# Six of eight experts take their tokens by an indirect DMA, one more weight chunk per expert stays unsplit, and the expert weights lie in runs of 8 KB

## What is computed

```
probs = softmax(LN(x) @ gate_w.T + gate_b)        # 8 experts
w_te  = the two largest probs of a token, else 0
per expert e:
    tok = the 93 tokens with the largest w_te[:, e]
    xg  = LN(x)[tok]                              # 93 x 512
    h   = gelu(xg @ w1[e] + b1[e])                # w1[e]: 512 x 2048
    y   = (h @ w2[e] + b2[e]) * w_te[tok, e]      # w2[e]: 2048 x 512
    x[tok] += y
```

## Time and profile before

| | us |
|---|---|
| runs | 2076.36, 2076.19, 2075.21 |
| profiled execution, its own time | 2075.6 |
| its span, first to last instruction | 2073.9 |
| TensorE (PE) busy | 2054.4 (99%) |
| VectorE (DVE) busy | 1485.4 (72%) |
| ScalarE (ACT) busy | 1139.5 (55%) |
| GpSimd (POOL) busy | 931.0 (45%) |
| granted TensorE clock | 1.000 |
| DMA | 201.15 MB, 97 GB/s over the span |

### The profile page before, as it was taken

The page is one execution under the profiler, slowest core; times in us unless marked ns, Lnnn a source line. Parts: engine busy times, 40 slices in busy tenths (PEclk is TensorE's granted clock), DMA queues, the critical chain, the costliest instruction groups (busy, mean ns, idle before and its releaser), DMA issues.

```text
span 2073.9 us, 36144 instructions
## 1 busy us (share of the span) xinstructions
PE 2054.4 (99%) x13385; PEld 1927.0 (93%) x13385; DVE 1485.4 (72%) x3088; ACT 1139.5 (55%) x3030; POOL 931.0 (45%) x707
## 2 busy tenths in 40 slices
PE   8999999999999999999999999999999999999998
PEld 7986666788899999999999999999999999999997
DVE  8769999744676766676767676676767676766776
ACT  4566777524655554555555555445555555554464
POOL 0010001301565655555555555555656565655461
PEclk9999999999999999999999999999999999999999
DMA  5205999900322111111122211111111222111110
GB/s 143 89 23 171 325 349 314 304 31 9 126 81 75 65 66 66 66 66 66 65 82 94 87 66 66 66 66 66 66 66 66 95 84 82 66 66 66 62 47 25
DMA packets 89162, 201.15 MB, mean 97 GB/s; under 512 B 8197, under 2 KB 12581, under 8 KB 88986
## 3 DMA queue, kind: packets, MB, share of 16 engines
q1 hardware_dynamic: 86746, 196.28, 27.7%
q0 software_dynamic: 2240, 2.57, 0.5%
HBM read 196.31 MB, written 2.51 MB: 96 GB/s over the span
## 4 chain that ended last, share of the span: by engine, by line
PE 95%; DVE 4%; ACT 1%; DMA 0%; issue 0%; POOL 0%; SPq 0%; DVEq 0%
PE PS L54 86%; PE PS L57 5%; PE PS L53 5%; DVE LW L60 1%; DVE JU L76 1%; DMA X<-in_x 0%; DVE OHsx L68 0%; DVE ACC L60 0%; DVE SM L107 0%; DVE XFL L60 0%; DVE OHdx L69 0%; DVE PO L68 0%; DVE U L69 0%; DVE W1L L60 0%; DVE GEL L60 0%
## 5 line engine op out<-in xcount | busy, mean ns | idle before, releaser
L54 PE MATMUL PS<-ZH,WS 128*128 128x314 f32 x4096 | 939.7, 310 | 0.0
L54 PEld LDWEIGHTS PS<-ZH,WS 128*128 128x128 f32 x4096 | 695.7, 189 | 0.0
L54 PE MATMUL PS<-ZL,WS 128*128 128x314 f32 x2048 | 626.9, 306 | 0.0
L60 DVE TENSOR_TENSOR ACC<-ACC,PS 128x314 f32<-128x314 f32 x1008 | 462.6, 476 | 196.9 <-PE PS L54 186.8
L60 POOL TENSOR_TENSOR WS<-RAW,WS 128x512 fp32r<-128x512 f32 x256 | 326.7, 1298 | 167.6 <-ACT WS L88 167.6
L54 PEld LDWEIGHTS PS<-ZL,WS 128*128 128x128 f32 x2048 | 387.0, 189 | 0.0
L60 POOL TENSOR_TENSOR ML<-MF,MH 128x400 fp32r<-128x400 f32 x124 | 129.7, 1046 | 428.5 <-ACT MH L88 428.5
L88 ACT ACTIVATE ZH<-PS,g1T 128x628 fp32r<-128x628 f32 x128 | 100.7, 787 | 255.0 <-PE PS L54 255.0
L60 POOL TENSOR_TENSOR WQ<-RAW,WQ 128x512 fp32r<-128x512 f32 x128 | 217.6, 1700 | 42.9 <-ACT WQ L88 42.9
L88 ACT ACTIVATE EE<-EE,SM 125x100 f32<-125x100 f32 x640 | 233.4, 379 | 1.2 <-DVE SM L68 1.2
L88 ACT ACTIVATE MH<-MF 128x400 fp32r<-128x400 f32 x128 | 68.3, 533 | 286.7 <-DVE MF L60 285.5
(11 more groups left out here) (366 smaller groups left out, 3650.1 us busy)
## 6 DMA issues: line engine op xcount, KB each, us to landing
RAW<-in_L_ffn_wz_w SPq DMA_DIRECT2D x66, 1024.0 KB, 5.3
RAW<-in_L_ffn_w SPq DMA_DIRECT2D x64, 1024.0 KB, 7.3
RAW<-in_L_ffn_Wq_w SPq DMA_DIRECT2D x32, 1024.0 KB, 5.5
CB<-c_rows SPq DMA_DIRECT2D x32, 195.3 KB
RAW<-in_L_gnn_W SPq DMA_DIRECT2D x4, 1024.0 KB, 16.1
RAW<-in_L_ffn_Wkv_w SPq DMA_DIRECT2D x4, 1024.0 KB, 15.1
RAW<-in_L_ffn_Wk_T SPq DMA_DIRECT2D x2, 1024.0 KB, 18.5
WB<-w_rows SPq DMA_DIRECT2D x6, 273.4 KB
```

The costliest lines, as they stand in the source:

```text
L54: return self.q.matmul(o, l, r, start=start, stop=stop)
L60: return Nothing() if self.q is None else self.q.tensor_tensor(out=o, in0=a, in1=b, op=op)
```

## The change

The diff, cut to its core; the tiles `XG` (94 x 2 x 512, over the place of `XFL`), `IX` and `TOK` are new.

```diff
-                srcs.append(I["L0_ffn_w1"][e, :, 512 * c:512 * c + 512].rearrange("(k p) n -> p k n", p=128))
+                srcs.append(I["L0_ffn_w1"][e, c])
-                srcs.append(I["L0_ffn_w2"][e, 512 * c:512 * c + 512, :].rearrange("(k p) n -> p k n", p=128))
+                srcs.append(I["L0_ffn_w2"][e, c])
...
-            return m % 8 < (7 if m < 8 * NE - 8 else 6)
+            return m % 8 < 6
...
-            return 7 * (m // 8) + m % 8
+            return 6 * (m // 8) + m % 8
...
@@ sp_moe, before the loop of loads
+            q.dma(xrow[0:1, :], ZR[:, :]).then_inc(s_wrow, 16)
+            q.wait_ge(*xfh_done.of(4, "u"))
+            for lo, hi in ((0, 120), (120, 125)):
+                q.dma(xrow[1:626, :].rearrange("(t p) d -> p t d", p=P)[lo:hi], MU[lo:hi, :, :]).then_inc(s_wrow, 16)
@@ g_moe
+            q.iota(TOK[:, :], [[P, T5]], 1).then_inc(*mconst.up("token"))
+            q.wait_ge(*mconst.of("token"))
+            q.ts(WSP[:, :, :, 2], TOK[:, :].unsqueeze(2).broadcast_to([P, T5, 8]), 1.0, None, ALU.add)
+            q.fill(WSP[:, :, :, 3].bitcast(f32), 0.0).then_inc(*mconst.up("code"))
...
+            q.wait_ge(s_wrow, 80)
+            for e in range(NP_, NE):
+                q.wait_ge(*sw_v.of(e, "row"))
+                q.wait_ge(*(xg_t.of(e - 2) if e >= NP_ + 2 else ga_mm.of(NP_ - 1)))
+                if e > NP_:
+                    q.wait_ge(s_rows, 16 * (e - NP_))
+                q.gather(XG[:, e % 2, :], xrow, IX[:, e % 2:e % 2 + 1]).then_inc(s_rows, 16)
+            q.wait_ge(s_rows, 16 * (NE - NP_))
@@ a_moe
-                q.wait_ge(*ga_mm.of(e))
-                q.act(OT[:, :], PS[0:CS, 6, :], ACT.Copy).then_inc(*ga_done.up(e))
+                if e < NP_:
+                    q.wait_ge(*ga_mm.of(e))
+                    q.act(OT[:, :], PS[0:CS, 6, :], ACT.Copy).then_inc(*ga_done.up(e))
...
             for e in range(NE):
-                n = 7 * e
+                n = 6 * e
...
-                weights(n + 10)
                 scale(e)
@@ v_moe
+            def places_of(e):
+                k = e % 2
+                q.wait_ge(*sw_mm.of(e))
+                if e > NP_ + 1:
+                    q.wait_ge(s_rows, 16 * (e - NP_ - 1))
+                q.cp(IX[:, k:k + 1], PS[0:CS, 4, 2:3]).then_inc(*sw_v.up(e, "row"))
...
                 q.wait_ge(*gelu_a.of(e, c))
+                q.wait_ge(s_wrow, 80)
...
             for e in range(NE):
-                n = 7 * e
+                n = 6 * e
+                if NP_ <= e + 1 < NE:
+                    places_of(e + 1)
                 weights(n + 4)
                 gelu(e, 0)
+                if NP_ <= e + 1 < NE:
+                    dispatch(e + 1)
...
-                if e == 0:
-                    gelu(e, 2)
-                if e and split(8 * e + 6):
-                    gelu(e, 2)
...
-                weights(n + 10)
@@ pe_moe, dispatch
+                if e >= NP_:
+                    return
...
+            def places_of(e):
+                k = e % 2
+                q.wait_ge(*rank_v.of(e, "po"))
+                q.wait_ge(*gate_v.of("wsl"))
+                q.wait_ge(*mconst.of("code"))
+                q.wait_ge(*free[4])
+                for t in range(T5):
+                    i = q.mm(PS[0:CS, 4, 0:4], PO2[:, k, t, :], WSP[:, t, e, :], t == 0, t == 4)
+                i.then_inc(*sw_mm.up(e))
+                free[4] = sw_v.of(e, "two")
@@ pe_moe, gathered_T
-                q.wait_ge(*ga_done.of(e))
+                if e < NP_:
+                    q.wait_ge(*ga_done.of(e))
+                else:
+                    q.wait_ge(s_rows, 16 * (e - NP_ + 1))
...
+                rows = OT[:, :] if e < NP_ else XG[:, e % 2, :]
...
             for e in range(NE):
+                if NP_ <= e + 1 < NE:
+                    places_of(e + 1)
                 up(e, 0)
@@ kernel, on the host
+        if name == "L0_ffn_w1":
+            a = _np.ascontiguousarray(a.reshape(8, 4, 128, 4, 512).transpose(0, 3, 2, 1, 4))
+        if name == "L0_ffn_w2":
+            a = _np.ascontiguousarray(a.reshape(8, 4, 4, 128, 512).transpose(0, 1, 3, 2, 4))
```

More of the change, by code:

```diff
@@ L1174, in program @@
         YH = at("YH", [P, T5, D], f32, after("HW3"))
+        XG = at("XG", [CS, 2, D], f32, after("XFH"))
+        IX = at("IX", [CS, 2], i32, after("XG"))
         LG = at("LG", [P, T5, 8], f32, after("XFL"))
@@ L1177, in program @@
         WM = at("WM", [P, T5, 8], f32, after("GS"))
-        WSP = at("WSP", [P, T5, 8, 2], f32r, after("WM"))
+        WSP = at("WSP", [P, T5, 8, 4], f32r, after("WM"))
         RKA = at("RKA", [P, 8, T5], f32, after("WSP"))
@@ L1183, in program @@
         IH = at("IH", [P, T5], i32, after("IL"))
-        c4 = at("c4", [P, 2, T5, 64], f32, after("IH"))
+        TOK = at("TOK", [P, T5], f32, after("IH"))
+        c4 = at("c4", [P, 2, T5, 64], f32, after("TOK"))
         CD = [at(f"CD{k}", [P, 6, T5], f32, after("IH") + 128 * k) for k in range(3)]
@@ L1243, in program @@
         wrow = nc.dram_tensor("w_rows", (8, 625), f32, kind="Internal").ap()
-        NB = 6
+        NB, NP_ = 6, 2
+        xrow = nc.dram_tensor("x_rows", (626, D), f32, kind="Internal").ap()
         yrow = nc.dram_tensor("y_rows", (1 + NB * CS, D), f32, kind="Internal").ap()
@@ L1322, in g_moe @@
             q.fill(io94[:, CAP:CS], -1.0).then_inc(*mconst.up("all"))
+            q.wait_ge(*mconst.of("all"))
+            q.iota(TOK[:, :], [[P, T5]], 1).then_inc(*mconst.up("token"))
+            q.wait_ge(*mconst.of("token"))
+            q.ts(WSP[:, :, :, 2], TOK[:, :].unsqueeze(2).broadcast_to([P, T5, 8]), 1.0, None, ALU.add)
+            q.fill(WSP[:, :, :, 3].bitcast(f32), 0.0).then_inc(*mconst.up("code"))
             q.wait_ge(*x1_done.of(4))
@@ L1577, in rank_end @@
                 if e >= 2:
-                    q.wait_ge(*ga_mm.of(e - 2))
+                    q.wait_ge(*sw_mm.of(e - 2))
+                    if e - 2 < NP_:
+                        q.wait_ge(*ga_mm.of(e - 2))
+                    if e - 2 >= NB:
+                        q.wait_ge(*pt_t.of(e - 2))
                 for t in range(T5):
@@ L1592, in dispatch @@
                     q.wait_ge(*os_hi.of(e - 2))
-                q.cp(sw[k][:, 0:2], PS[0:CS, 7, 0:2]).then_inc(*sw_v.up(e, "two"))
+                b = 7 if e < NP_ else 4
+                q.cp(sw[k][:, 0:2], PS[0:CS, b, 0:2]).then_inc(*sw_v.up(e, "two"))
                 q.wait_ge(*sw_v.of(e, "two"))
                 q.tt(sw[k][:, 2:3], sw[k][:, 0:1], sw[k][:, 1:2], ALU.add).then_inc(*sw_v.up(e, "sum"))
+            def places_of(e):
[4 more added lines that the diff above has]
+                q.cp(IX[:, k:k + 1], PS[0:CS, 4, 2:3]).then_inc(*sw_v.up(e, "row"))
             def gathered_T(e):
@@ L1614, in scale @@
                 q.wait_ge(s_b2[k], 32 * (e // 2 + 1))
-                q.wait_ge(*ga_done.of(e))
-                q.wait_ge(*xg_t.of(e))
-                if e + 1 < NE:
-                    q.wait_ge(*xg_t.of(e + 1))
+                q.wait_ge(*ga_done.of(NP_ - 1))
+                q.wait_ge(*xg_t.of(NP_ - 1))
+                if e:
+                    q.wait_ge(*os_hi.of(e - 1))
                 q.tt(OT[:, :], PS[0:CS, 2, :], B2[:, k, :], ALU.add).then_inc(*ot_v.up(e))
@@ L1654, in back_low @@
             def back_low():
-                q.wait_ge(s_rows, 16 * T5)
+                q.wait_ge(s_rows, 16 * (NE - NP_ + T5))
                 for t in range(T5):
@@ L1720, in v_moe @@
                     gathered_T(e + 1)
-                    dispatch(e + 1)
+                    if e + 1 < NP_:
+                        dispatch(e + 1)
                 weights(n + 9)
@@ L1751, in pe_moe @@
             q.wait_ge(*w_hi.of(0, 1))
-            pe_busy(q, 3, HW[1], 17)
+            pe_busy(q, 3, HW[0], 17)
             turned(0)
@@ L1874, in pe_moe @@
             q.wait_ge(*free[7])
-            pe_busy(q, 7, HW[1], 19)
+            pe_busy(q, 7, HW[0], 19)
             rank_row(0)
@@ L1878, in pe_moe @@
             q.wait_ge(*free[2])
-            pe_busy(q, 2, HW[1], 21)
+            pe_busy(q, 2, HW[0], 21)
             dispatch(0)
@@ L1966, in a_counts @@
         def a_counts(q):
-            q.wait_ge(*w_used.of(chunk(7 * NE - 4)))
+            q.wait_ge(*w_used.of(8 * NE - 5))
             for m in range(T5):
@@ L1972, in v_counts @@
             for m in range(T5):
-                q.wait_ge(*w_used.of(chunk(7 * NE - (3 if m < 4 else 2))))
+                q.wait_ge(*w_used.of(8 * NE - (4 if m < 4 else 3)))
                 q.wait_ge(*gch_done.of(m))
```

20 lines of the change are left out of this document (9 added, 11 removed).

## The result

The changed kernel took 2086.11 us, the median of six runs (2081.92 to 2090.87), against 2076.19 us (2075.21 to 2077.01) for the kernel before: a ratio of 1.0049, with a 95% interval of 1.0039 to 1.0059. It is 9.9 us slower. The forecast was 2067.0 us, and its range ended at 2073.0, so it was wrong in sign and in size. The profiled execution took 2087.79 us, with a span of 2086.0.

The account below looks back on a forecast made before the run. TensorE was taken to bound the kernel, with DMA and VectorE right behind. The terms -13.9 + 4.7 - 0.9 + 1.0 = -9.1 us against the profiled 2075.6 gave 2066.5, stated as a median of 2067.0; range 2064.5 to 2073.0.

Parts of the forecast that it names:

- What goes from TensorE, what comes: TensorE's order: gathering products go in experts 2 to 7 (13.9 us), chunk 6 unsplit in seven experts adds 4.7 us.
- the stall: First expert: PE's 0.87 us wait for XGL before expert 1's first product was taken as gone, 0.9 us saved.
- The gather: New indirect DMA of token rows: lands before the transposes need it, 0 us, bounds 0 and 1 us per expert.
- ScalarE's loads: Second rival: hidden tile 3's copy waits behind a high part whose chunk load lands late; 2083.6 us, chance 0.06.
- the rival's 17.5 us: Second rival's size: with landings of 11.8 us PE stops 2.5 us in each of seven experts; chance 0.06.
- Both ends: Start and end of the stage: new instructions, token writes and later loads stay hidden, 0 us, at worst 2 us each.
- The cover: End of the stage: Wk_T loads land 2.9 us before TensorE wants them, shrinking to some 1.3 us; 0, at worst 2.
- The granted clock: PE's clock was 1.00 in all windows, the 2.4 GHz level, and no change was expected.
- the tight point: DMA per expert: 9.24 MB need 26.7 us against a period of 25.6, or 25.1 us with the long-run layout.
- The 1.0 us of the sum: Loss over the whole stage for loads landing late on busy DMA; bounds 0 and 1.1 us for each of six experts.
- Third rival: The gather lands beyond T + 21.8 in the expert, so PE waits for it: 2074 to 2077 us, chance 0.05.
- The signs: Wrong if spacing exceeds 26.3 us, PE waits for HS, LW or XGL in each expert, or idles after 388 us for Wk_T or X.

Follow-up runs that it names:

- the kernel in which nothing is late: Changed kernel with gathers padded to 96 rows for XG and 128 for YL and YH, runs of 8 KB, chunk 6 unsplit: 2066.09 us, ratio 0.9945.
- the fastest kernel: Changed kernel with 96 rows for XG, 128 for YL and YH, and seven of eight chunks split as before the change: 2063.06 us, ratio 0.9939.

## Why the prediction was wrong, point by point

**What goes from TensorE, what comes: right.** The products taken out (13.9 us), the unsplit chunks (4.7) and the stall (0.9) make 10.1 us. 2076.2 - 10.1 = 2066.1, and the kernel in which nothing is late took 2066.09, with a period of 25.52 us for the 25.6 forecast. That it fits to 0.1 us is luck, since its parts are off by more: the unsplit chunk with its order cost 2.9 for 3.8, and the products, by the two kernels with chunk 6 unsplit and nothing waited for inside the experts, 2079.40 - 2066.09 = 13.3 for 13.9. The counts came as forecast: 128 records of RAW,GT in the stage (72 before), and products of XFH and XFL in experts 0 and 1 alone.

**The gather: the step that failed.** The prediction said "I take 0, bounds 0 and 1 us per expert". It priced the gather by its bytes ("0.19 MB is a seventh of five YH gathers"), as a smaller YH, and asked only when its own rows would be there. For the rows themselves that bound held in the changed kernel, even with a landing of 15.0 us: TensorE waits for no XG. What it left out is what the gather does to others while it lasts: 94 rows go to two DMA engines, with 47 rows each, as the packets show; the 1 MB loads in flight beside it land late, and the reading that fits is that they wait for their part on those engines. So 7.3 us became 10.1. The sum had nothing for this, and the row count, 2 x 47, was there to be asked about. Undoing this alone, by two rows, gives 13.9 us of the 19.

**ScalarE's loads: mechanism right, weight wrong.** It named the place (the copy of hidden tile 3 behind the high part), the allowance of 9.3 us from issue to landing and the landing from which the kernel would be slower, 10.7. The trace shows this wait in five experts; two of the loads behind them stand in the chain, with 9.36 and 10.45 us (a third, with 12.18, is behind a wait of 0.49 us for XGL, a fourth, with 9.49, behind the wait for PT). The allowance was a little too wide: with 9.36 us TensorE waited 1.20, with 10.45 it waited 2.29, so 8.2 us would have been in time in these two experts. It got a chance of 0.06, for the reason of the bytes above. The size is smaller than the rival's 17.5 us: 5.9 us of waits for HS, 1.2 in each of five experts, since the loads landed in some 10 us and not in 11.8. The rest came from the waits for PT, the lower clock and the end of the stage, which that rival did not price.

**Both ends: right at the start, wrong at the end.** "The cover shrinks to some 1.3 us but holds: 0, at worst 2 us." It didn't hold. `g_moe` lets the YL gathers start only when the last XG has landed, which the changed code adds; the trace shows it, 13.82 us of waiting:

```profile
360.64 1.93 POOL L125 DMA_INDIRECT YL<-y_rows,IL  x1 [13.82 <-DMA XG<-x_rows,IX]
```

YL thus started at 360.64, 5.4 us later than before (355.21 us), in a stage that should have ended 10 us earlier, and YH, of 125 rows, which go to 5 engines, took up to 25.1 us. The two together cost 5.07 us of idle time and 3.8 more with the clock, 8.9 in all. With the gathers at 128 rows the cover is there (YH 9.5 us).

**The granted clock, "I expect no change there": wrong.** It fell to its lower level, 1.2 GHz, after idle times of 2.29 us and 5.07 us (0.57 and 0.50 in the windows behind them), and cost some 1.7 us in the first place and 3.8 in the second. Not every wait carries this cost: behind one of 2.27 us the clock stayed at 1.00. No term of the sum had it.

**DMA: the tight point, and a milder one than feared.** The 1.0 us of the sum was not needed once the rows were padded: 9.24 MB fit into a period of 25.52 us, with windows of 356 to 367 GB/s at shares of 0.98 to 1.00. The Trainium skill, DMA: Bandwidth & Descriptors, "Specifications", gives about 358 GB/s of HBM per core; the windows of 364 and 370 GB/s over 26 us in the fastest kernel don't bear that out as a limit, though from 178 to 386 us the kernel with all gathers padded and chunk 6 unsplit moved 351 in the mean. That longer runs lower the share was right, but in the kernel before they are worth 0 us, in the changed one 7.1, with 96 rows -2.3 and with all gathers padded 3.8. Why they cost 2.3 there is only seen in part: YH, still at 125 rows, lands in 19.6 us beside long runs, against 12.5 beside short ones, which would be small packets held up on the queue behind large ones. That is argued, not shown, and the profiled execution with long runs was the faster one of the two.

**Third rival: not in the changed kernel, but in its neighbour.** It wanted a landing of 18 us, and the gathers of the changed kernel stayed at 16.5 or less. With seven of eight chunks split two of them took 17.9 and 18.7 us, and there TensorE waited for them, 5.1 us in all. The wait of 2.27 us in the changed kernel, which the trace puts down to YL at 370.16, is another thing: `gathered_T` waits for no YL. It also waits until bank 5 is free, which ScalarE's copy of PT does, and that ended at 370.01, late behind a high part that had waited 1.15 us for its load. So the late load has a part in it, 1.15 of the 2.27 us at most; where the rest comes from is open. This is read from the code and the times, and was not tried by itself.

**The signs.** Three of those by which the prediction called itself wrong are there: waits for HS, idle time after 388 us, and in its middle experts a spacing over 26.3 us (the five small products start at 231.20, 258.36 and 285.02, so 27.2 and 26.7 us apart).

## What to carry to other kernels

Ask how a gather's rows are dealt over the DMA engines before you price its bytes, and pad the row count to a multiple of 16 with unused rows (two rows of 2 KB were worth 13.9 us here). When a transfer is added beside a stream that is just on time, ask first what it does to the landings of that stream, and who reads them behind a narrow allowance. And work out what is held by the last piece of the new chain, here GpSimd's next gathers, before the old cover at the end of a stage is called enough.

## What the runs showed of the hardware that was not expected

A gather of 94 rows of 2 KB lands in 15.0 us, of 95 in 8.8, of 100 in 7.3 and of 96 in 6.5, beside the same stream of loads, and GpSimd's time to issue it is 1.48, 1.13, 1.01 and 0.92 us. For 125 rows against 128, in the kernel before, the landing is 11.8 against 7.2 us. A gather of 94 rows puts 400 packets on the queue, 48 of them with data; one of 96 rows puts 64, also 48 with data.

Two idle times of TensorE of nearly the same length had different effects on the granted clock in the changed kernel. Behind the wait of 2.29 us that ends at 303.73 it is 0.57 over the next 4 us, behind the one of 2.27 us that ends at 370.16 it stays at 1.00:

```profile
304.00:308.00 4.00, 4.00 (x14) 2.74 (x13) 3.96 (x7) 4.00 (x10) 0.00 (x0) 0.57 0.96 391
370.00:374.00 4.00, 3.84 (x13) 1.73 (x14) 2.77 (x3) 0.50 (x2) 2.30 (x3) 1.00 1.01 215
```
